# Decoder layer on one core: VectorE's share of the exponentials goes from 15 to 19 units a phase, by a quintic with a product made on GpSimd

## The chip, the cores and the metric

The kernel runs on one core of a Trainium2 chip. The metric is the device time of one execution in microseconds (us), as the median of several runs; lower is better.

## The reference

One decoder layer on `x` (1024 rows of 128) with a context `ctx` of 6404 rows of 128. Nearly all the time goes into the cross attention: 16 heads of depth 8, 1024 queries, 6404 keys.

```python
x = layernorm(x + attn(x, U))          # softmax(-|y_i - y_j|^2) @ x, y = x U
qh, kh, vh = heads(x @ Wq + bq), heads(ctx @ Wk + bk), heads(ctx @ Wv + bv)
attn = softmax(qh @ kh^T / sqrt(8))    # 16 x 1024 x 6404 exponentials
x = layernorm(x + (attn @ vh) @ Wo + bo)
x = layernorm(x + ffn_quantised(x))
```

## The kernel before

After a preparation (about 100 us: projections, keys split in three bf16 parts and written to DRAM), the attention runs in 8 **phases**: 4 groups of 4 heads times 2 halves of 512 queries. A phase walks over 17 **chunks** of 3 key tiles (`c` in 0 to 16). A chunk has 12 **units** of 128 keys x 512 queries, taken three at a time as 4 **blocks** (`t` or `s` in 0 to 3); the last chunk has 3 blocks, so a phase has 67. In this document "block 10" is the tenth after the phase's block 0, that is `c * 4 + t`.

For each block TensorE writes 3 units of scores into three of six PSUM banks (two sets, used in turn; `scores`, L1284), and ScalarE takes the exponential of the whole set in one instruction (`exponentials`, L710) into `probs`, a ring of 8 blocks in SBUF. TensorE later multiplies them with V, tile by tile (`values`, L1314). TensorE may start the scores of block b only when ScalarE has done block b-2, since both use the same banks (the wait on `probs_ready`).

One unit in some blocks isn't left to ScalarE: its instruction then covers 1024 columns and not 1536, and **VectorE** makes the third unit's exponentials by a polynomial. In the kernel before this is the third block (`E_BLOCK` is 2) of chunks 0 and 2 to 15: 15 units a phase. `take` rounds the scores (L960) and takes the fractional part (L966), both from PSUM; from then on the bank is free. `power` runs four steps of a polynomial (L979), then multiplies with a power of two and writes `probs` (L986). Every instruction covers 256 of the unit's 512 columns, so a unit is 14 instructions. **GpSimd** makes the power of two out of the rounded scores in one instruction (`powers`, L588), and copies V for each chunk into `v_op` (`stage`, L581), once TensorE has finished with the slot. VectorE waits at the end of a phase for the last values, adds and turns the accumulators (`add_acc`, `turn_acc`) and goes on. Each engine runs its own list in order; semaphores join them. SP's queue loads the keys for each chunk and the queries of each phase.

Of the kernel before, what the change touches and what calls it, by code (L numbers as in the profile page):

```python
# [22 lines left out]
F32 = mybir.dt.float32  # L23
# [6 lines left out]
P = 128  # L30
# [58 lines left out]

def decoder_layer(nc, x, ctx_in, U, Wq, bq, Wk, bk, Wv, bv, Wo, bo, clip_x, clip_down,  # L90
                  w_gate, w_up, w_down, out, score_limit=SCORE_LIMIT):
    stack = ExitStack()
    with stack:
# [64 lines left out]
        qf = sb("qf", [P, 2, HQ])  # L158
        qr = sb("qr", [P, 2, HQ])
# [41 lines left out]
        xq_t = sb("xq_t", [P, T], BF16)  # L201

# [34 lines left out]
        e_pow_ready = sem("e_pow_ready")  # L237
# [277 lines left out]
        def _(pool):  # L515
# [69 lines left out]
            def powers(ph, c):  # L585

                pool.wait_ge(e_step, E_STEPS * (e_count(ph, c) - 1) + 2)
                pool.tensor_scalar(e_pow[:], e_low(e_t[:]), float(2 ** 23), float(EXP2_LEAD),  # L588
                                   ALU.mult, ALU.add).then_inc(e_pow_ready, 1)

            for ph in range(PHASES):
                for c in range(NC):
                    m = ph * NC + c
                    stage(m % 2, m, c * CT, ph % NG * G)
                    if c != 1 and c < NC - 1:
                        powers(ph, c)
# [3 lines left out]
        def _(act):  # L600
# [113 lines left out]
            def shared(s):  # L714
                return BU * 512 - EW if s == E_BLOCK else BU * 512

            for ph in range(PHASES):
                f = ph * BPP
                for s in range(BPC):
                    exponentials(f + s, f + (s + 1 + AHEAD), shared(s))  # L720
                for s in range(BPC, 2 * BPC):
                    exponentials(f + s, f + (s + 1 + AHEAD))
                with act.Fori(0, E_UNITS // 2) as r:  # L723
                    for s in range(2 * BPC, 4 * BPC):
                        exponentials(f + s, r * (2 * BPC) + (f + s + 1 + AHEAD), shared(s % BPC))
# [788 lines left out]
```

## Time and profile before

| | |
|---|---|
| median of 3 runs | 834.43 us (834.39 to 834.64) |
| the profiled execution's own time | 833.03 us |
| its span (first to last instruction) | 831.3 us |
| busy in the span | TensorE 707.7, VectorE 689.5, ScalarE 736.0, GpSimd 174.9 us |
| one phase, start to start | 84.0 us |

The profiled execution is 1.4 us under the median of the runs; 1.7 us of it lie outside its span. Times in the views are from the span's start. A row that ends in "x6" in a timeline is six instructions merged, with the time from the first's start to the last's end.

### The profile page before, as it was taken

The numbers are of one execution on the slowest core, as the hardware profiler recorded it, in microseconds if no ns is written. First come the engines' busy times: TensorE is split into PE (matmuls) and PEld (weight loads), VectorE is DVE, ScalarE is ACT, GpSimd is POOL, SyncE is SP. The second block draws the span as 40 slices with busy tenths as digits, with TensorE's granted clock in tenths as the row PEclk, the third lists the DMA queues.
The fourth block names the chain that finished last, engine by engine and source line by source line (L and its number), as shares of the span: only waits on it lengthen the run. The fifth ranks groups of instructions, "written<-read, shape, count | busy, mean of one in ns | idle before, by whom it ended". The sixth has DMA issues, their size and how long they took to land.

```text
span 831.3 us, 38425 instructions
## 1 busy us (share of the span) xinstructions
PE 707.7 (85%) x15210; PEld 319.9 (38%) x15212; DVE 689.5 (83%) x1952; ACT 736.0 (89%) x650; POOL 174.9 (21%) x304
## 2 busy tenths in 40 slices
PE   6996679899899998899998999888899998899841
PEld 3445434443444344334443444344433443344321
DVE  3518767996999699969996999699978997899766
ACT  2436879999999999999999999999999999999741
POOL 2501511221222122212221222122212221222100
PEclk9998989999999999999999999999999999999965
DMA  3303521111111111111111111111111111111000
GB/s 105 83 25 107 170 86 37 37 43 44 38 36 45 42 37 38 43 43 38 36 44 43 36 37 40 44 38 35 40 48 35 37 37 49 37 36 38 14 1 26
DMA packets 36611, 38.41 MB, mean 46 GB/s; under 512 B 8430, under 2 KB 35088, under 8 KB 36512
## 3 DMA queue, kind: packets, MB, share of 16 engines
q1 hardware_dynamic: 35644, 36.59, 14.8%
q8 instruction: 65, 1.06, 0.5%
q10 hardware_dynamic: 868, 0.48, 0.2%
q14 instruction: 34, 0.28, 0.1%
HBM read 30.15 MB, written 6.42 MB: 44 GB/s over the span
## 4 chain that ended last, share of the span: by engine, by line
ACT 40%; issue 24%; PE 16%; SPq 10%; DVE 5%; DMA 3%; POOL 1%; ACTq 1%; POOLq 0%; DVEq 0%
ACT probs L710 39%; SPq L291 8%; PE ps L1314 6%; PE ps L1284 3%; PE ps L1213 2%; PE ps L1199 2%; DMA k_op<-k_parts_dram 2%; SPq L505 1%; DMA k_parts_dram<-k_parts 1%; PE ps L1162 1%; DVE stats L776 1%; PE ps L1449 1%; ACTq L723 1%; POOL k_parts L541 0%; DMA q_parts_dram<-q_parts 0%
## 5 line engine op out<-in xcount | busy, mean ns | idle before, releaser
L710 ACT ACTIVATE probs<-ps 128x1536 f32<-128x1536 f32 (+1 forms) x536 | 671.7, 1379 | 11.9 <-PE ps L1284 11.4
L1314 PE MATMUL ps<-probs,v_op 64*9 64x512 f32 (+1 forms) x8384 | 523.5, 494 | 13.8 <-DMA k_op<-k_parts_dram 9.1
L1284 PE MATMUL ps<-q_op,k_op 59*32 59x512 bf16 x6432 | 337.4, 382 | 60.7 <-ACT probs L710 56.4
L979 DVE SCALAR_TENSOR_TENSOR e_u<-e_u,e_f 128x256 f32<-128x256 f32 x720 | 259.2, 425 | 0.0
L1284 PEld LDWEIGHTS ps<-q_op,k_op 59*32 59x32 bf16 x6432 | 107.9, 90 | 331.5 <-issue 245.7
L1314 PEld LDWEIGHTS ps<-probs,v_op 64*9 64x9 f32 x8384 | 169.3, 86 | 90.2 <-issue 27.7
L588 POOL TENSOR_SCALAR e_pow<-e_t 128x512 int32<-128x512 int16 x120 | 74.4, 620 | 353.9 <-DVE e_t L960 353.9
L960 DVE TENSOR_SCALAR e_t<-ps 128x256 f32<-128x256 f32 x240 | 90.5, 418 | 60.5 <-PE ps L1284 51.3
L581 POOL COPY v_op<-v_all 128x108 f32<-128x108 f32 x136 | 68.3, 502 | 181.3 <-PE ps L1314 180.6
L979 DVE SCALAR_TENSOR_TENSOR e_u<-e_f 128x256 f32<-128x256 f32 x240 | 90.1, 416 | 0.2
L986 DVE SCALAR_TENSOR_TENSOR probs<-e_u,e_pow 128x256 f32<-128x256 f32 x240 | 89.6, 411 | 0.0
L966 DVE SCALAR_TENSOR_TENSOR e_f<-ps,e_t 128x256 f32<-128x256 f32 x240 | 89.2, 413 | 0.0
L541 POOL TENSOR_TENSOR k_parts<-probs,k_parts 128x384 bf16<-128x384 f32 x17 | 17.6, 1038 | 66.2 <-ACT k_parts L640 66.2
L667 ACT ACTIVATE probs<-ps,neg_n 128x1024 f32<-128x1024 f32 x8 | 8.9, 1113 | 16.8 <-PE ps L1213 16.8
L1162 PE MATMUL ps<-ctx_t,wk_turned 128*128 128x384 f32 x34 | 16.6, 571 | 6.3 <-ACT ctx_t L619 3.3
L1009 DVE STREAM_TRANSPOSE att_rows<-acc_t 128x512 f32<-128x512 f32 x7 | 5.0, 711 | 15.6 <-DMA o_t<-att_rows 15.6
L627 ACT ACTIVATE kf<-ps,bias_cols 128x384 f32<-128x384 f32 x17 | 9.8, 578 | 8.9 <-PE ps L1162 8.9
L1165 PEld LDWEIGHTS ps<-wv_sb,ctx_t 128*128 128x128 f32 x102 | 15.5, 208 | 5.2 <-issue 1.2
L1213 PE MATMUL ps<-y_rhs,y_lhs 64*128 64x512 f32 x32 | 15.6, 611 | 0.7 <-DVE v_all L811 0.7
L811 DVE TENSOR_TENSOR v_all<-ps,bv_bc 128x384 f32<-128x384 f32 (+1 forms) x17 | 9.4, 555 | 7.8 <-PE ps L1165 7.8
L640 ACT ACTIVATE k_parts<-probs 128x384 bf16<-128x384 f32 x17 | 8.8, 519 | 8.0 <-DVE probs L826 8.0
L1199 PE MATMUL ps<-probs,x_nat 128*128 128x512 f32 x32 | 15.6, 615 | 0.0
(177 smaller groups left out, 257.7 us busy)
## 6 DMA issues: line engine op xcount, KB each, us to landing
k_op<-k_parts_dram SPq DMA_DIRECT2D x544, 36.0 KB
k_parts_dram<-k_parts SPq DMA_DIRECT2D x17, 288.0 KB, 2.5
k_op<-k_parts_dram SPq DMA_DIRECT2D x272, 12.0 KB
ctx_nat<-in_ctx_dram SPq DMA_DIRECT2D x16, 192.0 KB, 2.6
q_op<-q_parts_dram SPq DMA_DIRECT2D x32, 48.0 KB
q_parts_dram<-q_parts SPq DMA_DIRECT2D x2, 384.0 KB, 3.4
x_nat<-in_x_dram SPq DMA_DIRECT2D x1, 512.0 KB, 3.9
o_t<-att_rows SPq DMA_DIRECT2D x28, 16.0 KB
```

Source lines behind the costliest of these rows:

```text
L291: sp.dma_start(k_op[W2 * r + a:W2 * r + a + DH * copies, slot, :, :].rearrange("p i t -> p (i t)"), bass.AP(src.tensor, starts[part][r], [ ...
L581: pool.tensor_copy(v_op[:, slot].rearrange("p j (h d) -> p j h d", h=G), v_all[:, bass.ds(tile, CT), head:head + G, :]).then_inc(v_staged, 1)
L588: pool.tensor_scalar(e_pow[:], e_low(e_t[:]), float(2 ** 23), float(EXP2_LEAD), ALU.mult, ALU.add).then_inc(e_pow_ready, 1)
L710: act.activation(probs[:, b % NP].rearrange("p u t -> p (u t)")[:, 0:columns], ps[:, bank:bank + BU, :].rearrange("p u t -> p (u t)")[:, 0 ...
L960: dve.tensor_scalar(e_t[:, cols], score, E_MIN, ROUND, ALU.max, ALU.add).then_inc(e_step, 1)
L966: dve.scalar_tensor_tensor(out=e_f[:, cols], in0=score, scalar=E_MIN, in1=e_low(e_t[:, cols]), op0=ALU.max, op1=ALU.subtract).then_inc(e_s ...
L979: dve.scalar_tensor_tensor(out=e_u[:, cols], in0=u[:, cols], scalar=a, in1=e_f[:, cols], op0=ALU.add, op1=ALU.mult).then_inc(e_step, 1)
L986: dve.scalar_tensor_tensor(out=probs[:, block % NP, BU - 1, 512 - EW + cols.start:512 - EW + cols.stop], in0=e_u[:, cols], scalar=EXP2[0], ...
L1199: last = pe.matmul(ps[:, 4 + b, :], x_nat[:, j, :], attn_e[:, j, HQ * b:HQ * b + HQ], start=(j == 0), stop=(j == TQ - 1), skip_group_check ...
L1213: last = pe.matmul(ps[:, 2 * (j % 2) + b, :], y_lhs[:, P * j:P * j + P], y_rhs[:, HQ * b:HQ * b + HQ], start=True, stop=True)
L1284: return pe.matmul(ps[a:a + P // G, bank, :], k_op[W2 * r:W2 * r + KR, kslot, i, P * j + a:P * j + a + P // G], q_op[W2 * r:W2 * r + KR, q ...
L1314: last = pe.matmul(ps[32 * k:32 * k + DH + 1, ACC[h], a:b], v_op[W2 * h:W2 * h + W2, slot, j, (DH + 1) * k:(DH + 1) * (k + 1)], probs[W2 * ...
```

## The change

The polynomial is another one, and its work is divided anew. With f the fraction and u0 = f + EXP2[0], GpSimd makes u = u0 * f, a quadratic; VectorE makes f' = (u + EXP2[2]) * f (`cube`), then f'' = (f' + EXP2[3]) * 2^n and (u + EXP2[1]) * f'' (`power`, now two steps). A unit is 10 VectorE instructions of 256 columns (was 14) and 3 GpSimd instructions of 512 (was 1): the power of two, `u0`, and the product, which reads two tiles. `e_f`, `e_u` and `e_pow` are doubled (the second set lies in `q_work`), `e_t` isn't.

A phase has 19 units, at the blocks listed by `E_AT`: block 0; then in each turn of 4 chunks, from chunk 2, blocks 2, 5, 8, 11 and 14 of the turn's 16; and blocks 58, 61 and 64. VectorE runs `take` of unit n, `power` of unit n-1, `cube` of unit n, and so on. TensorE reads values two chunks back for tile 2 and half of tile 1, one chunk back for the rest, and waits for the unit's semaphore `e_probs` where it reads it; before the scores of block b it waits for `e_taken` of a unit in block b-2.

```diff
+E_TURN = ((0, 2), (1, 1), (2, 0), (2, 3), (3, 2))
+E_AT = ([(0, 0)] + [(c + k, t) for c in range(E_FIRST, NC - 3, E_LOOP) for k, t in E_TURN] +
+        [(NC - 3, 2), (NC - 2, 1), (NC - 1, 0)])
...
-            def powers(ph, c):
-
-                pool.wait_ge(e_step, E_STEPS * (e_count(ph, c) - 1) + 2)
-                pool.tensor_scalar(e_pow[:], e_low(e_t[:]), float(2 ** 23), float(EXP2_LEAD),
+            def powers(ph, c, t):
+
+                n = e_count(ph, c, t)
+                f, u, pow2 = e_f[n % 2], e_u[n % 2], e_pow[n % 2]
+                if n > 2:
+
+                    pool.wait_ge(e_probs, E_AHEAD + 2 * (n - 2))
+                pool.wait_ge(e_rounded, 2 * n)
+                pool.tensor_scalar(pow2, e_low(e_t[:]), float(2 ** 23), float(EXP2_LEAD),
                                    ALU.mult, ALU.add).then_inc(e_pow_ready, 1)
+                pool.wait_ge(e_taken, 2 * n)
+                pool.tensor_scalar(u, f, EXP2[0], None, ALU.add).then_inc(e_square_ready, 1)
+                pool.wait_ge(e_square_ready, 2 * n - 1)
+                pool.tensor_tensor(u, u, f, ALU.mult).then_inc(e_square_ready, 1)
...
+            def cube(ph, c, t):
+
+                n = e_count(ph, c, t)
+                f, u = e_f[n % 2], e_u[n % 2]
+                dve.wait_ge(e_square_ready, 2 * n)
+                for cols in halves:
+                    dve.scalar_tensor_tensor(out=f[:, cols], in0=u[:, cols], scalar=EXP2[2],
+                                             in1=f[:, cols], op0=ALU.add, op1=ALU.mult
                                              ).then_inc(e_step, 1)
...
-                for i, a in enumerate(reversed(EXP2[1:])):
-                    u = e_f if i == 0 else e_u
-                    for n, cols in enumerate(halves):
...
+                for i, cols in enumerate(halves):
+                    dve.wait_ge(e_step, done + i + 1)
+                    dve.scalar_tensor_tensor(out=f[:, cols], in0=f[:, cols], scalar=EXP2[3],
+                                             in1=pow2[:, cols].bitcast(F32), op0=ALU.add, op1=ALU.mult
+                                             ).then_inc(e_step, 1)
+                for i, cols in enumerate(halves):
+                    dve.wait_ge(e_step, done + 2 + i + 1)
+                    dve.scalar_tensor_tensor(out=probs[:, block % NP, BU - 1, cols], in0=u[:, cols],
+                                             scalar=EXP2[1], in1=f[:, cols], op0=ALU.add, op1=ALU.mult
+                                             ).then_inc(e_probs, 1)
...
+                for n, at in enumerate(E_AT):
+                    take(ph, *at)
+                    if n > 1:
+                        power(ph, *E_AT[n - 1])
+                    elif n == 0 and ph:
+                        power(ph - 1, *E_AT[-1])
+                    cube(ph, *at)
...
+                    if c or s >= 2:
+                        wait_unit(e_taken, 0, ph, *((c, s - 2) if s >= 2 else (c - 1, s + 2)))
...
+                    elif s == 0:
+                        made(2, 1, a=HQ // 2)
+                    elif s == 1:
+                        made(2, 2)
+                    elif s == 2:
...
+                        made(1, 0, first=c == 1)
                     else:
-                        values(slot, f - BPC, 1, False, a=(s - 1) * (HQ // 2), b=s * (HQ // 2))
+                        made(1, 1, b=HQ // 2)
```

VectorE's list, one unit in the middle of a phase, before:

```order
L960 TENSOR_SCALAR e_t<-ps 128x256 [waits scores_done]
L960 TENSOR_SCALAR e_t<-ps 128x256
L966 SCALAR_TENSOR_TENSOR e_f<-ps,e_t 128x256 [waits e_step] x2
L979 SCALAR_TENSOR_TENSOR e_u<-e_f 128x256 [waits e_step] x2
L979 SCALAR_TENSOR_TENSOR e_u<-e_u,e_f 128x256 [waits e_step] x6
L986 SCALAR_TENSOR_TENSOR probs<-e_u,e_pow 128x256 [waits e_pow_ready,e_step] x2
```

The same place now, from one `take` to the next (`q_work` is the second set of the work tiles):

```order
L987 TENSOR_SCALAR e_t<-ps 128x256 [waits scores_done,e_pow_ready]
L987 TENSOR_SCALAR e_t<-ps 128x256
L991 SCALAR_TENSOR_TENSOR e_f<-ps,e_t 128x256 [waits e_rounded] x2
L1013 SCALAR_TENSOR_TENSOR q_work<-q_work 128x256 [waits e_step] x2
L1018 SCALAR_TENSOR_TENSOR probs<-q_work 128x256 [waits e_step] x2
L1001 SCALAR_TENSOR_TENSOR e_f<-e_u,e_f 128x256 [waits e_square_ready]
L1001 SCALAR_TENSOR_TENSOR e_f<-e_u,e_f 128x256
L987 TENSOR_SCALAR e_t<-ps 128x256 [waits scores_done,e_pow_ready]
```

The next `take` stands behind the `cube`, whose first instruction waits for GpSimd's product (`e_square_ready`); before, nothing between two takes waited for more than the power of two.

GpSimd's list in the middle of a phase, two chunks before:

```order
L581 COPY v_op<-v_all 128x108 [waits values_done,v_ready]
L588 TENSOR_SCALAR e_pow<-e_t 128x512 [waits e_step]
L581 COPY v_op<-v_all 128x108 [waits values_done,v_ready]
L588 TENSOR_SCALAR e_pow<-e_t 128x512 [waits e_step]
```

And now, two units:

```order
L591 COPY v_op<-v_all 128x108 [waits values_done,v_ready]
L603 TENSOR_SCALAR e_pow<-e_t 128x512 [waits e_rounded,e_probs]
L606 TENSOR_SCALAR e_u<-e_f 128x512 [waits e_taken]
L608 TENSOR_TENSOR e_u<-e_u,e_f 128x512 [waits e_square_ready]
L591 COPY v_op<-v_all 128x108 [waits values_done,v_ready]
L603 TENSOR_SCALAR q_work<-e_t 128x512 [waits e_rounded,e_probs]
L606 TENSOR_SCALAR q_work<-q_work 128x512 [waits e_taken]
L608 TENSOR_TENSOR q_work<-q_work 128x512 [waits e_square_ready]
```

Two instructions of 512 columns have come into each unit, and the second waits for the first's semaphore.

TensorE's list now, around the last block of one turn of four chunks and the first of the next (L1320 are scores, L1350 values; the registers' instructions carry the waits):

```order
L1363 REGISTER_ALU [waits e_taken,consts_ready]
L1320 MATMUL ps<-q_op,k_op 32x512 [waits probs_ready,consts_ready]
L1320 MATMUL ps<-q_op,k_op 32x512 x11
L1350 MATMUL ps<-probs,v_op 9x256 x8
L1363 REGISTER_ALU
L1320 MATMUL ps<-q_op,k_op 32x512 [waits probs_ready,consts_ready]
L1320 MATMUL ps<-q_op,k_op 32x512 x11
L1350 MATMUL ps<-probs,v_op 9x512 [waits e_probs,consts_ready]
L1350 MATMUL ps<-probs,v_op 9x512 x7
```

The same place before, where a chunk's last block ends with tile 2 of the chunk before:

```order
L1284 MATMUL ps<-q_op,k_op 32x512 [waits probs_ready,consts_ready]
L1284 MATMUL ps<-q_op,k_op 32x512 x11
L1327 REGISTER_ALU
L1314 MATMUL ps<-probs,v_op 9x512 [waits e_probs,consts_ready]
L1314 MATMUL ps<-probs,v_op 9x512 x7
L1327 REGISTER_ALU
L1327 REGISTER_ALU [waits e_step,consts_ready]
L1284 MATMUL ps<-q_op,k_op 32x512 [waits probs_ready,consts_ready]
```

The wait for a unit's values (`e_probs`) has moved from the chunk's fourth block to the second block of the chunk after, and stands between the scores of blocks 1 and 2.

## Rows read from the trace of the kernel before

**Rows 1.** The page's first part: busy time of each engine over the span.
```profile
PE 707.7 (85%) x15210; PEld 319.9 (38%) x15212; DVE 689.5 (83%) x1952; ACT 736.0 (89%) x650; POOL 174.9 (21%) x304
```

**Rows 2.** Windows: one stretch of 67 us inside the second phase.
```profile
core 0: us, PE busy (x) PEld busy (x) DVE busy (x) ACT busy (x) POOL busy (x), PEclk, DMA share, GB/s
198.00:265.00 67.00, 60.28 (x1524) 27.23 (x1512) 63.22 (x183) 66.94 (x54) 14.46 (x26) 1.00 0.13 38
```

**Rows 3.** Waits over the whole span: engine line, releaser: us in total, times, longest.
```profile
PE ps L1284 <- ACT probs L710: 56.4, 214, 1.4
DVE e_t L960 <- PE ps L1284: 51.3, 19, 6.1
```

**Rows 4.** Timeline of ScalarE: start, length, then the instruction; four in a row.
```profile
216.93 1.45 ACT L710 ACTIVATE probs<-ps 128x1536 f32<-128x1536 f32 x1
218.26 1.47 ACT L710 ACTIVATE probs<-ps 128x1536 f32<-128x1536 f32 x1
219.59 1.05 ACT L710 ACTIVATE probs<-ps 128x1024 f32<-128x1024 f32 x1
220.53 1.45 ACT L710 ACTIVATE probs<-ps 128x1536 f32<-128x1536 f32 x1
```

**Rows 5.** Timeline of VectorE: one unit and the start of the next.
```profile
219.19 0.76 DVE L960 TENSOR_SCALAR e_t<-ps 128x256 f32<-128x256 f32 x2
219.86 0.74 DVE L966 SCALAR_TENSOR_TENSOR e_f<-ps,e_t 128x256 f32<-128x256 f32 x2
...
221.19 2.17 DVE L979 SCALAR_TENSOR_TENSOR e_u<-e_u,e_f 128x256 f32<-128x256 f32 x6
223.28 0.75 DVE L986 SCALAR_TENSOR_TENSOR probs<-e_u,e_pow 128x256 f32<-128x256 f32 x2
224.13 0.76 DVE L960 TENSOR_SCALAR e_t<-ps 128x256 f32<-128x256 f32 x2
```

**Rows 6.** Timeline of GpSimd beside that unit.
```profile
220.03 0.62 POOL L588 TENSOR_SCALAR e_pow<-e_t 128x512 int32<-128x512 int16 x1 [2.90 <-DVE e_t L960]
221.56 0.51 POOL L581 COPY v_op<-v_all 128x108 f32<-128x108 f32 x1 [0.92 <-PE ps L1314]
```

**Rows 7.** Single lines: durations in ns as min/median/max, first and last start.
```profile
L581 POOL COPY v_op<-v_all x136: 272/517/2602, 102.7 to 779.9; 128x108 f32<-128x108 f32 x136
L541 POOL TENSOR_TENSOR k_parts<-probs,k_parts x17: 906/919/1296, 21.1 to 99.3; 128x384 bf16<-128x384 f32 x17
L826 DVE TENSOR_TENSOR probs<-kf,k_parts x17: 542/548/1124, 17.2 to 98.1; 128x384 f32<-128x384 f32 x17
```

**Rows 8.** Timeline of the preparation: a GpSimd and a VectorE instruction that overlap.
```profile
68.13 0.91 POOL L541 TENSOR_TENSOR k_parts<-probs,k_parts 128x384 bf16<-128x384 f32 x1 [31.93 <-ACT k_parts L640]
68.33 1.12 DVE L826 TENSOR_TENSOR probs<-kf,k_parts 128x384 f32<-128x384 f32 x1
```

**Rows 9.** Timeline of both engines in the seventh phase: the longest copy.
```profile
634.09 2.60 POOL L581 COPY v_op<-v_all 128x108 f32<-128x108 f32 x1 [0.84 <-PE ps L1314]
633.80 2.09 DVE L979 SCALAR_TENSOR_TENSOR e_u<-e_u,e_f 128x256 f32<-128x256 f32 x6
635.81 0.74 DVE L986 SCALAR_TENSOR_TENSOR probs<-e_u,e_pow 128x256 f32<-128x256 f32 x2
```

**Rows 10.** Groups of GpSimd: busy us, mean ns, idle before.
```profile
L588 POOL TENSOR_SCALAR e_pow<-e_t 128x512 int32<-128x512 int16 x120 | 74.4, 620 | 353.9 <-DVE e_t L960 353.9
L554 POOL MEMSET k_op<- 128x3072 bf16 x1 | 2.7, 2727 | 0.0
L571 POOL TENSOR_TENSOR x_bo<-x,bo_bc 128x1024 f32<-128x1024 f32 x1 | 2.4, 2357 | 0.0
```

**Rows 11.** Timeline of VectorE: the first unit of the third and of the fourth phase, and the second unit of the third.
```profile
277.54 0.76 DVE L960 TENSOR_SCALAR e_t<-ps 128x256 f32<-128x256 f32 x2 [4.13 <-PE ps L1284]
...
288.25 0.75 DVE L960 TENSOR_SCALAR e_t<-ps 128x256 f32<-128x256 f32 x2 [1.73 <-PE ps L1284]
...
361.55 0.76 DVE L960 TENSOR_SCALAR e_t<-ps 128x256 f32<-128x256 f32 x2 [4.14 <-PE ps L1284]
```

**Rows 12.** Timeline of TensorE: scores, a full tile of values, the next scores.
```profile
219.87 0.61 PE L1284 MATMUL ps<-q_op,k_op 59*32 59x512 bf16 x12 [0.30 <-ACT probs L710]
220.14 1.21 PE L1314 MATMUL ps<-probs,v_op 64*9 64x512 f32 x16
221.05 0.61 PE L1284 MATMUL ps<-q_op,k_op 59*32 59x512 bf16 x12
```

More of the change, by code:

```diff
@@ L593, in _ @@
                     m = ph * NC + c
-                    stage(m % 2, m, c * CT, ph % NG * G)
-                    if c != 1 and c < NC - 1:
-                        powers(ph, c)
+                    for t in range(BPC):
+                        if t == 2:
+                            stage(m % 2, m, c * CT, ph % NG * G)
+                        if (c, t) in E_AT:
+                            powers(ph, c, t)
         @block.scalar
@@ L712, in exponentials, with chunk @@
                                ACT.Exp, scale=1.0 / LOG2E).then_inc(probs_ready, 1)
-            def shared(s):
-                return BU * 512 - EW if s == E_BLOCK else BU * 512
-            for ph in range(PHASES):
[L718 to L725, printed above, removed]
-                for s in range((NC - 1) * BPC, BPP):
-                    exponentials(f + s, f + (s + 1 + AHEAD))
+            def chunk(ph, c, i=None):
+                f = ph * BPP + c * BPC
+                for t in range(LAST_BPC if c == NC - 1 else BPC):
+                    count = f + t + 1 + AHEAD
+                    exponentials(f + t, count if i is None else i * (E_LOOP * BPC) + count,
+                                 BU * 512 - EW if (c, t) in E_AT else BU * 512)
+            for ph in range(PHASES):
+                for c in range(E_FIRST):
+                    chunk(ph, c)
+                with act.Fori(0, (NC - 3 - E_FIRST) // E_LOOP) as i:
+                    for c in range(E_FIRST, E_FIRST + E_LOOP):
+                        chunk(ph, c, i)
+                for c in range(NC - 3, NC):
+                    chunk(ph, c)
             act.wait_ge(pe_tail, TAIL_ATT_T)
@@ L1326, in at @@
                 def at(count, step):
-                    return count if i is None else pe.to_reg(i * (reach * step) + count)
+                    return count if i is None else pe.to_reg(i * step + count)
                 def wait(signal, count):
@@ new lines, in made @@
+                def made(back, j, a=0, b=HQ, count=1, first=False):
+                    ph_v, c_v = (ph, c - back) if c >= back else (ph - 1, c - back + NC)
+                    if ph_v < 0:
+                        return
+                    if j == 0:
+                        wait(v_staged, at(m - back + 1, KS))
+                    if a == 0:
+                        for t in range(BPC):
+                            if (t * BU + BU - 1) // G == j:
+                                wait_unit(e_probs, E_AHEAD, ph_v, c_v, t)
+                    values((m - back) % 2, ph_v * BPP + c_v * BPC, j, c_v == NC - 1, count, first, a, b)
@@ L1358, in chunk @@
+                    if c == 0:
+                        if s < 2:
+                            made(2, s + 1, count=2 - s)
+                        else:
+                            made(1, s - 2, count=s - 1)
+                    elif c == 1 and s < 2:
+                        if s == 0:
+                            made(2, 2)
                     elif s == 0:
+                        made(2, 1, a=HQ // 2)
+                    elif s == 1:
+                        made(2, 2)
+                    elif s == 2:
@@ L1387, in project_out @@
                 last.then_inc(pe_tail, 1)
+            last_m = PHASES * NC - 1
+            pe.wait_ge(e_probs, E_AHEAD + 2 * (E_UNITS * PHASES - 1))
+            for j in range(1, CT):
+                values((last_m - 1) % 2, BLOCKS - LAST_BPC - BPC, j, False, count=3 - j)
             pe.wait_ge(o_written, 16 * G * NG)
```

136 lines of the change are left out of this document (62 added, 74 removed).

## The prediction

> **What bounds the kernel now.** I read the page's busy times first [rows 1]: ScalarE, TensorE and VectorE lie close together, so a share of the span decides nothing. The windows show the inside of a phase [rows 2]: ScalarE is busy for 66.94 of 67.00 us, VectorE 63.22, TensorE 60.28, GpSimd 14.46, TensorE's granted clock 1.00, the upper of its levels, 2.4 GHz. The waits say the same from the other side [rows 3]: TensorE's scores wait for ScalarE 214 times, VectorE waits for scores 19 times, mostly at a phase's start. So ScalarE bounds every phase. Its pace is in the timeline [rows 4]: starts 1.33 us apart behind an instruction of 1536 columns, 0.94 behind one of 1024. A unit taken from it saves 0.39 us. VectorE is just behind: a unit of 14 instructions every 4.94 us, 0.335 us each [rows 5]. GpSimd's two instructions in that time cost nothing [rows 6].
>
> **What the change removes.** Four more units a phase leave ScalarE: 4 x 0.39 = 1.56 us a phase, 12.5 us over 8 phases, if ScalarE stays the bound. VectorE goes from 15 x 14 = 210 to 19 x 10 = 190 instructions a phase, so by count it has room too.
>
> **What it adds: a chain through GpSimd.** Between two takes VectorE must now pass the cube, which waits for a GpSimd product made from this unit's fraction. The time from take to take can't be less than this chain. With ScalarE as the bound there are, over three blocks with one shortened, 2 x 1.33 + 0.94 = 3.6 us for it, and from block 14 to 18 4.94 us.
>
> The two new GpSimd instructions have no row of their own. The product: two-input instructions took 2.36 us for 1024 columns and 0.91 (the undisturbed ones) for 384, 2.27 ns a column, so 512 take 0.91 + 0.29 = 1.20 us [rows 7, 10]. The addition of a constant: nearest is the power of two, 0.62 us for the same 512 columns [rows 10]. Bounds: a memset's rate, 2.73 us for 3072 columns, gives 0.45 below; the two-input price 1.20 above. I take 0.62.
>
> The GPSIMD Engine Reference of the Trainium skill (section 3.1) gives one-input bodies 1.03 cycles an element, about 0.44 us for 512 at its 1.2 GHz, as an estimate; the trace's 0.62 for such an instruction is longer. By the page's figure the sum below would be 26 us less.
>
> **What the two engines do to each other.** VectorE's instruction with two SBUF inputs took 0.55 us alone and 1.12 when a GpSimd instruction had started 0.2 us before it: that ended at 69.04, VectorE's at 69.45, as if it had begun when GpSimd ended, 0.41 us for 384 columns, so 0.27 for 256 [rows 7, 8]. The other way round, the copy takes 0.27 alone and 0.52 beside the polynomial's steps, and the six steps around it take 2.17 instead of 2.09 [rows 5, 6, 7, 9]. So a VectorE instruction that reads two SBUF tiles and a GpSimd instruction that reads SBUF exclude each other for nearly their whole length. In before this cost 0.08 us a chunk. After, cube and power (six instructions a unit) read two SBUF tiles, and so they exclude GpSimd's 0.62 and 1.20. Only take, which reads PSUM, runs beside GpSimd, and GpSimd's addition can't start until take is done.
>
> The copy's 0.27 kept VectorE out for some 0.15 (0.08 lost, and the gap of 0.335 - 0.27 used), so I count 0.12 us less than a GpSimd instruction's length as exclusion. The cycle, in order: take 4 x 0.335 = 1.34; power's first 0.33, in which GpSimd's addition becomes ready (fraction seen at 1.42, start 0.08 later as behind the rounding [rows 5, 6]) and waits; addition 0.50; power's second 0.27; product 1.08; power's last two and cube's two, 4 x 0.335 = 1.34. That is 4.86. The copy of V, now in four of five units, becomes ready while GpSimd is in the product and then takes its turn among these: 0.8 x 0.08 = 0.06. **4.9 us a unit.** That is above the 3.6 us, and above the 4.94 us only where four blocks lie between. So VectorE with GpSimd sets the pace, ScalarE waits.
>
> Two more waits follow. (1) power of unit n ends 4.2 us after take of n+1. TensorE reads unit 11 of a turn in block 17, before the scores of block 18. Its scores of block 16 follow take of block 14 (1.42 + 0.1 + 0.6 = 2.1), those of 17 at 3.0, then it waits to 4.2, values 0.6, scores 0.6 [rows 12]: take of block 18 at 5.5 and not 4.9. 0.6 us, three times a phase. (2) At a phase's start block 64's values are read after the scores of block 2, so again at 4.2 behind take of block 0; values 0.6, scores 0.6: 5.4; ScalarE runs six blocks to 5.4 + 6 x 1.34 = 13.4, scores 0.6: the second unit (block 10) is taken 14.0 us after the first. VectorE's work on the accumulators, some 4 us, lies inside.
>
> **Sum.** From block 10 to the next phase's block 0 there are 18 intervals of 4.9 = 88.2, plus 3 x 0.6 = 1.8, plus 14.0: 104.0 us. Before: 84.0 [rows 11]. +20.0 a phase, 160 over 8. At the end the last unit's power and two tiles of values come behind ScalarE's end: +3. Against the profiled execution's 833.0: 996; the median was 1.4 above it: **998 us**. The 12.5 us of ScalarE are in this sum as nothing: it is idle for about a fifth of the phase.
>
> **Bounds.** Addition at 0.45, copy free, neither of the two extra waits: 18 x 4.67 + 12.1 = 96.2, gives 934. Addition at 1.20 gives 1082.
>
> **Rivals.** (a) *GpSimd starved.* One copy took 2.60 us: it waited until eight back-to-back steps had ended [rows 7, 9]. If GpSimd's addition isn't let in between power's four instructions, the cycle is 1.34 + 1.34 + 0.50 + 0.2 + 1.08 + 0.1 + 0.67 = 5.23, a phase 110, the time 1047. Against it: the median copy, 0.52, got in after one step. The SBUF — State Buffer page of the Trainium skill (section "SBUF: two separate sides") says that whichever starts first holds the shared pair for its whole instruction and the other blocks; by that a waiting GpSimd instruction goes next. The 2.60 us copy doesn't agree, the median does. 0.12.
>
> (b) *No exclusion for these shapes.* Then 1.42 + 0.08 + 0.62 + 0.09 + 1.20 + 0.09 + 0.67 = 4.17 us; 18 x 4.17 + 12.1 = 87.2, +3.2 a phase: 861. It still loses since 4.17 is over ScalarE's average, (84.0 - 13.0) / 18 = 3.94 at break-even. Against it stands [rows 8]. 0.08.
>
> (c) *Faster.* GpSimd's two instructions take together less than 3.94 - 2.35 = 1.59 us, undisturbed (mine are 1.82), so ScalarE stays the bound and the 12.5 us come: 822. Needs both (b) and faster instructions than any row. 0.04. That the product saves VectorE nothing at all, no change: 0.01.
>
> (d) *More than I counted*: the addition at its upper price, or TensorE at 1.2 GHz for stretches, since it would be busy 60.3 x 84 / 104, some 73% of a window where it now has 90% at clock 1.00 [rows 2]. Values and scores would then lengthen both extra waits. 0.08, 1065 and up.
>
> **Chances.** The ledger with GpSimd let in between (934 to 1035): 0.67; (a) 0.12; (d) 0.08; (b) 0.08; (c) 0.04; no change 0.01. The range 920 to 1065 holds the first two and a little of (d). This kernel's runs differ by 0.03%, so 0.2% is what can be told from no change. Faster 0.04, same 0.01, slower 0.95.
>
> **What would show it.** VectorE's takes 4.9 us apart inside a phase; idle time of ScalarE behind TensorE's scores of some 20 us a phase, and those waiting for VectorE's fraction; VectorE's step behind the product of 1.2 us or more instead of 0.42; GpSimd's addition near 0.75 with its wait, its product near 1.2; GpSimd about 2.5 us busy a unit. The forecast is wrong if VectorE's steps keep 0.42 us beside GpSimd's product, if the product takes under 1 us, or if takes follow each other in 3.6 us.

## The result, and the profile after

| | before | after |
|---|---|---|
| median | 834.53 us (834.39 to 834.76, 4 runs) | 1025.91 us (1023.92 to 1028.12, 4 runs) |
| profiled execution, its span | 833.03, 831.3 us | 1023.92, 1022.2 us |
| first takes of phases, apart | 90.0, then 83.9 to 85.6 us | 108.4 to 109.0 us |

The ratio is 1.229, with an interval of 1.2266 to 1.2313. Slower was forecast, with 998 us in 920 to 1065; the time lies 28 us above the forecast.

The page's first part, the answer to [rows 1], and its fourth, the shares of the chain that ended last:

```profile
PE 749.9 (73%) x15212; PEld 314.0 (31%) x15212; DVE 704.5 (69%) x1792; ACT 742.8 (73%) x650; POOL 591.9 (58%) x640
...
POOL 38%; DVE 27%; PE 19%; issue 9%; ACT 6%; POOLq 0%; DVEq 0%; ACTq 0%
```

No engine is above 73% now, and yet GpSimd, the least busy of the four, holds the most of the chain. That is how a round trip between two engines looks on a page: neither is full, since each stands while the other works. The windows say it of 60 us inside one phase (columns as in [rows 2], where ScalarE was busy all the time):

```profile
340.00:400.00 60.00, 44.91 (x1036) 18.67 (x1036) 44.70 (x114) 45.59 (x37) 42.37 (x44) 0.94 0.09 27
```

The waits, answering to [rows 3] (us in total, times, longest), name the round trip and its followers:

```profile
ACT probs L731 <- PE ps L1320: 189.0, 167, 2.2
DVE q_work L1001 <- POOL q_work L608: 110.1, 76, 3.1
DVE e_f L1001 <- POOL e_u L608: 108.4, 76, 3.1
PE ps L1320 <- DVE q_work L991: 87.4, 65, 2.2
PE ps L1320 <- DVE e_f L991: 83.0, 65, 2.0
PE ps L1350 <- DVE probs L1018: 21.2, 42, 1.3
```

VectorE's cube (L1001) waits 218.5 us for GpSimd's product, in all 152 units, 1.44 us each. TensorE's scores wait 170 us for the take that stands behind that cube, and ScalarE waits 189 us for the scores. It is one wait told three times. The two timelines show one unit whole, VectorE first:

```profile
401.41 0.74 DVE L987 TENSOR_SCALAR e_t<-ps 128x256 f32<-128x256 f32 x2
402.07 0.74 DVE L991 SCALAR_TENSOR_TENSOR q_work<-ps,e_t 128x256 f32<-128x256 f32 x2
402.74 1.21 DVE L1013 SCALAR_TENSOR_TENSOR e_f<-e_f,e_pow 128x256 f32<-128x256 f32 x2
403.87 0.75 DVE L1018 SCALAR_TENSOR_TENSOR probs<-e_u,e_f 128x256 f32<-128x256 f32 x2
405.95 0.80 DVE L1001 SCALAR_TENSOR_TENSOR q_work<-q_work 128x256 f32<-128x256 f32 x2 [1.33 <-POOL q_work L608]
```

and GpSimd beside it:

```profile
402.31 0.62 POOL L603 TENSOR_SCALAR q_work<-e_t 128x512 int32<-128x512 int16 x1 [1.44 <-DVE e_t L987]
403.01 1.55 POOL L606 TENSOR_SCALAR q_work<-q_work 128x512 f32<-128x512 f32 x1
404.64 1.28 POOL L608 TENSOR_TENSOR q_work<-q_work 128x512 f32<-128x512 f32 x1
```

The addition (L606) starts 1.60 us after the take, behind the power of two that is in GpSimd's way until then. It takes 1.55 us, not the 0.62 that I had counted. Then 0.08, the product 1.28, 0.03, and the cube's 0.72 up to the next take: 1.60 + 1.55 + 0.08 + 1.28 + 0.03 + 0.72 = **5.26 us**, the distance of takes inside a phase. The power's four instructions (L1013, L1018) end at 404.62, beside the addition, and VectorE stands idle while the product runs. Over the whole span the addition's mean is 1.54 us and the product's 1.28, 152 of each.

Takes in VectorE's timeline, answering to [rows 11]: the first unit of the first, the third, the fourth and the last phase, and the second unit of the third:

```profile
101.76 0.74 DVE L987 TENSOR_SCALAR e_t<-ps 128x256 f32<-128x256 f32 x2
...
319.10 0.74 DVE L987 TENSOR_SCALAR e_t<-ps 128x256 f32<-128x256 f32 x2
...
333.04 0.75 DVE L987 TENSOR_SCALAR e_t<-ps 128x256 f32<-128x256 f32 x2 [3.58 <-PE ps L1320]
...
427.75 0.74 DVE L987 TENSOR_SCALAR e_t<-ps 128x256 f32<-128x256 f32 x2
...
862.83 0.74 DVE L987 TENSOR_SCALAR e_t<-ps 128x256 f32<-128x256 f32 x2
```

The third phase is 108.65 us long: 13.94 to the second unit, then 18 intervals of 5.26 on average; the three over four blocks are 5.30 to 5.32. (In the last phase the second unit comes 15.4 us after the first, in the first 13.7.)

The first and the last phase of the kernel before began here:

```profile
103.65 0.76 DVE L960 TENSOR_SCALAR e_t<-ps 128x256 f32<-128x256 f32 x2 [0.98 <-PE ps L1284]
...
700.98 0.76 DVE L960 TENSOR_SCALAR e_t<-ps 128x256 f32<-128x256 f32 x2 [4.82 <-PE ps L1284]
```

So seven phases took 597.3 us before and 761.1 after, +163.7; the first take came 1.9 us earlier, and from the last phase's first take to the end it went from 130.3 to 159.4, +29.1. Together +190.9, all of the difference of the two profiled executions.

### The profile page after: what moved, and what is told of

The parts are those of the page before. It is cut to its first block, busy times and chain, and to the rows that moved or that the text cites. A ratio compares the mean times of both kernels' runs of the same rounds, so it can differ in the third digit from the quotient of the medians.

```text
span 1022.2 us, 38544 instructions
## 1 busy us (share of the span) xinstructions
PE 749.9 (73%) x15212; PEld 314.0 (31%) x15212; DVE 704.5 (69%) x1792; ACT 742.8 (73%) x650; POOL 591.9 (58%) x640
## 4 chain that ended last, share of the span: by engine, by line
POOL 38%; DVE 27%; PE 19%; issue 9%; ACT 6%; POOLq 0%; DVEq 0%; ACTq 0%
DVE e_t L987 10%; POOL q_work L606 9%; POOL e_u L606 8%; PE ps L1350 8%; POOL q_work L608 7%; POOL e_u L608 7%; ACT probs L731 5%; PE ps L1320 4%; POOL q_work L603 3%; DVE e_f L1001 3%; POOL e_pow L603 3%; DVE q_work L1001 3%; DVE probs L1018 2%; PE ps L1249 1%; PE ps L1235 1%
## 5 line engine op out<-in xcount | busy, mean ns | idle before, releaser
L1350 PE MATMUL ps<-probs,v_op 64*9 64x512 f32 (+1 forms) x8384 | 546.1, 516 | 23.0 <-DVE probs L1018 21.2
L1320 PE MATMUL ps<-q_op,k_op 59*32 59x512 bf16 x6432 | 352.5, 397 | 200.8 <-DVE q_work L991 87.4
L1320 PEld LDWEIGHTS ps<-q_op,k_op 59*32 59x32 bf16 x6432 | 117.0, 93 | 480.5 <-issue 355.1
L1350 PEld LDWEIGHTS ps<-probs,v_op 64*9 64x9 f32 x8384 | 166.8, 89 | 137.8 <-issue 73.1
L1001 DVE SCALAR_TENSOR_TENSOR q_work<-q_work 128x256 f32<-128x256 f32 x152 | 60.7, 438 | 110.1 <-POOL q_work L608 110.1
L1001 DVE SCALAR_TENSOR_TENSOR e_f<-e_u,e_f 128x256 f32<-128x256 f32 x152 | 60.7, 438 | 108.4 <-POOL e_u L608 108.4
L606 POOL TENSOR_SCALAR q_work<-q_work 128x512 f32<-128x512 f32 x76 | 117.3, 1544 | 6.0
L606 POOL TENSOR_SCALAR e_u<-e_f 128x512 f32<-128x512 f32 x76 | 117.3, 1543 | 6.0
L608 POOL TENSOR_TENSOR e_u<-e_u,e_f 128x512 f32<-128x512 f32 x76 | 97.1, 1278 | 6.3
L608 POOL TENSOR_TENSOR q_work<-q_work 128x512 f32<-128x512 f32 x76 | 97.0, 1277 | 6.3
L1013 DVE SCALAR_TENSOR_TENSOR q_work<-q_work 128x256 f32<-128x256 f32 x152 | 90.7, 635 | 0.0
L1013 DVE SCALAR_TENSOR_TENSOR e_f<-e_f,e_pow 128x256 f32<-128x256 f32 x152 | 90.2, 632 | 0.0
L1018 DVE SCALAR_TENSOR_TENSOR probs<-e_u,e_f 128x256 f32<-128x256 f32 x152 | 56.7, 411 | 0.0
L1018 DVE SCALAR_TENSOR_TENSOR probs<-q_work 128x256 f32<-128x256 f32 x152 | 56.7, 411 | 0.0
L991 DVE SCALAR_TENSOR_TENSOR q_work<-ps,e_t 128x256 f32<-128x256 f32 x152 | 56.2, 408 | 0.0
```

The costliest lines, as they stand in the source:

```text
L606: pool.tensor_scalar(u, f, EXP2[0], None, ALU.add).then_inc(e_square_ready, 1)
L608: pool.tensor_tensor(u, u, f, ALU.mult).then_inc(e_square_ready, 1)
L991: dve.scalar_tensor_tensor(out=f[:, cols], in0=ps[:, bank, cols], scalar=E_MIN, in1=e_low(e_t[:, cols]), op0=ALU.max, op1=ALU.subtract).th ...
L1001: dve.scalar_tensor_tensor(out=f[:, cols], in0=u[:, cols], scalar=EXP2[2], in1=f[:, cols], op0=ALU.add, op1=ALU.mult).then_inc(e_step, 1)
L1013: dve.scalar_tensor_tensor(out=f[:, cols], in0=f[:, cols], scalar=EXP2[3], in1=pow2[:, cols].bitcast(F32), op0=ALU.add, op1=ALU.mult).then ...
L1018: dve.scalar_tensor_tensor(out=probs[:, block % NP, BU - 1, cols], in0=u[:, cols], scalar=EXP2[1], in1=f[:, cols], op0=ALU.add, op1=ALU.mu ...
```

## Experiments

Two things were open: why the addition takes 1.55 us, and whether the two engines exclude each other at all, since the cycle of 5.26 adds up without it. On the addition: either it is the price of this form of instruction, or VectorE keeps it out. On the cycle: exclusion is real but hidden, because the power lies beside the slow addition; or there is none, and the chain's lengths are all; or VectorE's own work bounds it. Each experiment ran beside the kernel before on the same chip: 832.38 us (one run) for the first four, 834.96, 835.28 and 835.13 (medians of 14 to 17 runs) for the others. The first four and e10 have one run each; their differences are read inside the timelines. Where a run's text names one interval of takes, it is the usual one inside a phase.

**e1_prices**: the disputed prices by themselves. Behind the end of the kernel before, GpSimd runs a row of instructions of 512 columns, twice with VectorE idle, twice beside a stream of VectorE steps that read two SBUF tiles.

```diff
+                priced.step(pool.tensor_scalar(pb, pa, 28.2, None, ALU.add))
+                priced.step(pool.tensor_scalar(pb, pa, 28.2, 1.5, ALU.add, ALU.mult))
+                priced.step(pool.tensor_scalar(pb, pa, 28.2, 1.5, ALU.mult, ALU.add))
+                priced.step(pool.tensor_scalar(pb, pa, 28.2, None, ALU.mult))
+                priced.step(pool.tensor_tensor(pc, pb, pa, ALU.mult))
+                priced.step(pool.tensor_tensor(pc, pa, pa, ALU.mult))
...
```

> The kernel before, with a price list behind its end: when all its work is done, GpSimd runs eleven instructions of 512 columns on spare tiles, each waiting for the one before, twice with VectorE idle and twice beside 60 VectorE instructions of 256 columns that read two SBUF tiles. Its time means nothing. Theory S (the new addition is slow by itself): the addition of a constant to 512 f32 columns takes about 1.5 us with VectorE idle, the product about 1.27. Theory X (the prediction's: the addition is as short as the power of two, and is kept waiting by VectorE): the addition takes about 0.6 us alone and 1.5 only beside VectorE's stream. Both: the int16 to int32 form takes 0.62.

Its time, 891.41 us, says nothing, as the work is added. The timeline of GpSimd, VectorE idle, in the order of the diff (L608 to L613; the third, 0.62 us too, is left out):

```profile
827.82 1.50 POOL L608 TENSOR_SCALAR v_all<-v_all 128x512 f32<-128x512 f32 x1 [44.96 <-DVE res L816]
829.41 0.62 POOL L609 TENSOR_SCALAR v_all<-v_all 128x512 f32<-128x512 f32 x1
...
830.81 1.50 POOL L611 TENSOR_SCALAR v_all<-v_all 128x512 f32<-128x512 f32 x1
832.39 1.26 POOL L612 TENSOR_TENSOR v_all<-v_all 128x512 f32<-128x512 f32 x1
833.73 1.04 POOL L613 TENSOR_TENSOR v_all<-v_all 128x512 f32<-128x512 f32 x1
```

The first of them beside VectorE's stream, the stream's first 12 steps beside GpSimd, and its last 25, when GpSimd has ended:

```profile
851.97 1.66 POOL L608 TENSOR_SCALAR v_all<-v_all 128x512 f32<-128x512 f32 x1 [0.20 <-POOL v_all L618]
...
851.86 9.23 DVE L1160 SCALAR_TENSOR_TENSOR v_all<-v_all 128x256 f32<-128x256 f32 x12 [24.20 <-POOLq L623]
...
877.75 11.47 DVE L1160 SCALAR_TENSOR_TENSOR v_all<-v_all 128x256 f32<-128x256 f32 x25
```

A scalar instruction with one operation takes 1.50 us, with two operations 0.62, in either order. I had taken the price of the power of two, which has two. Beside VectorE's stream each of them is only 0.04 to 0.16 longer (the product 1.35): contention doesn't explain 1.55. The stream itself, in which each step waits for the one before, gets 12 steps in 9.23 us, 0.77 each; once GpSimd has ended they follow 0.46 apart. So the two engines do keep each other out, and it is VectorE that pays. Step by step: the one under way beside a scalar instruction takes 0.71 us and not 0.42, whether that instruction is the long or the short one, and the next two beside the long one take 0.42 again; beside a product of two tiles a step takes 1.37. The long scalar instruction keeps VectorE out no longer than the short one.

**e2_no_add**: GpSimd makes u = f * f; the addition of EXP2[0] is left out of the computation.

```diff
-                pool.tensor_scalar(u, f, EXP2[0], None, ALU.add).then_inc(e_square_ready, 1)
-                pool.wait_ge(e_square_ready, 2 * n - 1)
-                pool.tensor_tensor(u, u, f, ALU.mult).then_inc(e_square_ready, 1)
+                pool.tensor_tensor(u, f, f, ALU.mult).then_inc(e_square_ready, 2)
```

> The changed kernel without GpSimd's addition: the product is f * f, so the polynomial lacks one coefficient. Takes now 5.26 us apart. If a serial chain alone set the pace (fraction, addition, product, cube) it would be 5.26 - 1.63 = 3.63 us, ScalarE would be the bound again and the time 820 to 830. If exclusion counts as well: the product can't run beside power's last three instructions, so 1.34 + 0.39 + 1.15 + 5 x 0.335 = 4.55 us a unit, a phase 95.8, the time about 928. Theory X with an addition of 0.6 us and 0.9 us of waiting: about 4.6, the same 930.

913.45 us. VectorE, then GpSimd, in one unit:

```profile
407.87 0.76 DVE L985 TENSOR_SCALAR e_t<-ps 128x256 f32<-128x256 f32 x2 [0.15 <-PE ps L1318]
...
409.20 1.65 DVE L1011 SCALAR_TENSOR_TENSOR q_work<-q_work 128x256 f32<-128x256 f32 x2
...
412.19 0.74 DVE L985 TENSOR_SCALAR e_t<-ps 128x256 f32<-128x256 f32 x2
...
409.48 1.09 POOL L606 TENSOR_TENSOR e_u<-e_f 128x512 f32<-128x512 f32 x1
```

The square again starts 1.61 us after the take. By the chain alone the next take could follow at 1.61 + 1.09 + 0.03 + 0.72 = 3.45, under ScalarE's three blocks; it follows at 4.32. The power's first two instructions take 1.65 us instead of 0.74: the second waits until the square ends. So with the addition gone the exclusion shows. 110 us of the profiled 1023.92 come back, near what was expected with exclusion (928 us in all, 4.55 a unit) and far from the 820 to 830 of the chain alone.

**e3_one_step**: the power's first step is left out (the factor 2^n with it); two VectorE instructions a unit less.

```diff
-E_STEPS = 4
+E_STEPS = 2
...
-                    dve.scalar_tensor_tensor(out=f[:, cols], in0=f[:, cols], scalar=EXP2[3],
-                                             in1=pow2[:, cols].bitcast(F32), op0=ALU.add, op1=ALU.mult
-                                             ).then_inc(e_step, 1)
```

> The changed kernel with power's first step (the multiplication with the power of two) left out, so VectorE has 8 instructions a unit and two fewer that exclude GpSimd; the output lacks that factor. Theory S: VectorE's steps lie beside the slow addition, the cycle stays at 5.2 and the time at 1015 to 1026. Theory X: GpSimd's addition and product get in earlier, 5.26 - 0.67 = 4.6 us, the time about 930.

1025.73 us, nothing gained, and takes still 5.27 apart:

```profile
403.07 0.74 DVE L987 TENSOR_SCALAR e_t<-ps 128x256 f32<-128x256 f32 x2
...
407.62 0.80 DVE L1001 SCALAR_TENSOR_TENSOR q_work<-q_work 128x256 f32<-128x256 f32 x2 [2.01 <-POOL q_work L608]
408.34 0.74 DVE L987 TENSOR_SCALAR e_t<-ps 128x256 f32<-128x256 f32 x2
```

The cube's wait grew from 1.33 to 2.01 us, by the 0.67 that was cut. VectorE's own work is not the bound.

**e4_late_cube**: the cube of unit n stands behind the take of unit n+1, so that the chain no longer lies between two takes.

```diff
+                        cube(ph, *E_AT[n - 1])
...
-                    cube(ph, *at)
```

> The changed kernel with the cube of unit n moved behind the take of unit n+1, in front of its power: all work stays, only the serial chain from take to take is cut. Without exclusion GpSimd's own work would be the bound, 0.62 + 1.55 + 1.28 + 0.22 + waits 0.3 = 4.0 us a unit, the time about 845. With exclusion of the parts in which GpSimd reads (0.5 + 0.66 + 1.15 + 0.12) and VectorE's six two-input instructions (2.0) it is 4.4 to 4.6 us, the time about 925. If the addition excludes VectorE for its whole length, 5.3 us or more, the time about 1030. Theory X expects about 4.6.

1024.29 us, where a large gain was expected: a miss. Over three blocks the cycle does fall, to 4.88, but not over four:

```profile
399.62 0.74 DVE L987 TENSOR_SCALAR e_t<-ps 128x256 f32<-128x256 f32 x2
...
404.50 0.74 DVE L987 TENSOR_SCALAR e_t<-ps 128x256 f32<-128x256 f32 x2
...
407.63 1.82 DVE L1018 SCALAR_TENSOR_TENSOR probs<-q_work 128x256 f32<-128x256 f32 x2
411.12 0.76 DVE L987 TENSOR_SCALAR e_t<-ps 128x256 f32<-128x256 f32 x2 [1.67 <-PE ps L1323]
```

A unit's values are now ready later, 4.95 us after the next take, and TensorE waits for them before it writes the next scores: 6.62 us here, and 15.7 at the phase's start. These are the two extra waits of the prediction; the first had been small in the kernel after (5.3 over four blocks), the second is longer than its 13.94. They take back the 0.38 that each shorter interval gives: phases are 108.6 to 109.6 us long (the first 106.3), against 108.4 to 109.0. Taking the chain off one path put its length on another.

**e5_two_op**: the addition gets a second operation that does nothing, a multiplication by 1.

```diff
-                pool.tensor_scalar(u, f, EXP2[0], None, ALU.add).then_inc(e_square_ready, 1)
+                pool.tensor_scalar(u, f, EXP2[0], 1.0, ALU.add, ALU.mult).then_inc(e_square_ready, 1)
```

> The changed kernel with one edit: GpSimd's addition gets a second operation, a multiplication by 1.0, since in the price list that form took 0.62 us and the form with one operation 1.49. All values stay the same. If only the serial chain counts: 5.26 - 0.93 = 4.33 us a unit and about 915 us. If exclusion counts as in the prediction's ledger (power's second instruction waits for the addition, its last two and the cube for the product): 4.75 to 4.9 us a unit, about 990 us.

1016.39 us (1012.49 to 1022.93, 4 runs), 1.2163 times the kernel before (1.2084 to 1.2243). GpSimd and VectorE in one unit:

```profile
407.08 0.67 POOL L606 TENSOR_SCALAR e_u<-e_f 128x512 f32<-128x512 f32 x1
407.83 1.32 POOL L608 TENSOR_TENSOR e_u<-e_u,e_f 128x512 f32<-128x512 f32 x1
...
400.50 0.74 DVE L987 TENSOR_SCALAR e_t<-ps 128x256 f32<-128x256 f32 x2
...
405.48 0.74 DVE L987 TENSOR_SCALAR e_t<-ps 128x256 f32<-128x256 f32 x2
...
407.94 1.83 DVE L1018 SCALAR_TENSOR_TENSOR probs<-q_work 128x256 f32<-128x256 f32 x2
...
411.43 0.76 DVE L987 TENSOR_SCALAR e_t<-ps 128x256 f32<-128x256 f32 x2 [0.99 <-PE ps L1320]
```

The addition lost 0.88 us, the cycle only 0.29 (4.98 from 400.50 to 405.48). The product now falls on the power's last two instructions, which take 1.83 us and not 0.75, and the cube no longer waits at all. This is the unit as the prediction drew it, and its 4.9 us is 0.08 short of it. The time was still missed: with exclusion about 990 us had been expected. As the power ends later, TensorE's wait for values has grown from 21.2 us in 42 waits to this:

```profile
PE ps L1350 <- DVE probs L1018: 128.7, 112, 2.4
```

Over four blocks the interval is 5.95 to 6.06 (5.3 in after), the second unit mostly comes 16.5 us after the first (13.94), and a phase is 107 to 108.5 us. So the shorter cycle is mostly lost again outside it.

**e10_two_op_one_step** puts e3's cut on top of e5, to separate exclusion from chain (again without the factor 2^n).

> e5 (the addition with two operations) with power's first step left out, the same cut that changed nothing in e3 (the output lacks the power of two). If exclusion between power and the product sets e5's 4.97 us, the cut takes two VectorE instructions of 0.335 us off the path: 4.3 us a unit inside a turn and about 930 us. If only the serial chain counted, the cut would change nothing again: 4.97 us and about 1010 us.

904.18 us; takes 4.44 apart:

```profile
402.97 0.74 DVE L987 TENSOR_SCALAR e_t<-ps 128x256 f32<-128x256 f32 x2
...
406.69 0.80 DVE L1001 SCALAR_TENSOR_TENSOR e_f<-e_u,e_f 128x256 f32<-128x256 f32 x2 [1.17 <-POOL e_u L608]
407.41 0.74 DVE L987 TENSOR_SCALAR e_t<-ps 128x256 f32<-128x256 f32 x2
```

The same two instructions were worth nothing in e3 and 0.54 us a unit here, and 112 us in all with the shorter waits for values. A chain by itself can't do that: in e5 the power stood in the product's way, in e3 it had a gap. Hidden exclusion is what both runs fit; 4.44 is also what the chain alone adds up to here (1.61 + 0.67 + 0.08 + 1.33 + 0.03 + 0.72).

**e6_vector_product**: VectorE makes (f + EXP2[0]) * f itself, in one instruction per half; GpSimd keeps only the power of two. Still 19 units; 12 instructions a unit.

```diff
-                pool.tensor_scalar(u, f, EXP2[0], None, ALU.add).then_inc(e_square_ready, 1)
-                pool.wait_ge(e_square_ready, 2 * n - 1)
-                pool.tensor_tensor(u, u, f, ALU.mult).then_inc(e_square_ready, 1)
...
+                    dve.scalar_tensor_tensor(out=u[:, cols], in0=f[:, cols], scalar=EXP2[0],
+                                             in1=f[:, cols], op0=ALU.add, op1=ALU.mult
+                                             ).then_inc(e_square_ready, 1)
```

> The changed kernel with the same polynomial, but VectorE makes the product itself, in two instructions (f + a) * f; GpSimd is left with the power of two. 12 VectorE instructions a unit, 19 units. Both theories: no wait for GpSimd is left, 12 x 0.335 = 4.02 to 4.1 us a unit, over ScalarE's 3.9 on average, so some 855 us (848 to 865): two VectorE instructions cost less than the wait for GpSimd, but 19 units are still too many.

866.79 us (865.71 to 867.28, 4 runs), 2 us over the range expected; ratio 1.0359 (1.0303 to 1.0415). Two takes:

```profile
406.61 0.76 DVE L983 TENSOR_SCALAR e_t<-ps 128x256 f32<-128x256 f32 x2 [0.86 <-PE ps L1322]
...
410.68 0.74 DVE L983 TENSOR_SCALAR e_t<-ps 128x256 f32<-128x256 f32 x2
```

Two VectorE instructions, 0.67 us, do what cost 1.1 us of blocked VectorE or 1.4 us of waiting. So 159 of the 191 us lie in GpSimd's having the addition and the product. What is left is VectorE's own pace, 4.07 to 4.13 us for three blocks in which ScalarE needs 3.6.

**e7 to e11** look for a version that gains. All have 16 units a phase, mostly four blocks apart, where ScalarE gives VectorE 4.94 us (at block 2 of chunks 0 and 2 to 15 and block 1 of chunk 16). TensorE also gets one more wait, behind chunk 1, for the values of the phase's first unit.

```diff
-E_TURN = ((0, 2), (1, 1), (2, 0), (2, 3), (3, 2))
+E_TURN = ((0, 2), (1, 2), (2, 2), (3, 2))
...
-         [(NC - 3, 2), (NC - 2, 1), (NC - 1, 0)])
+         [(NC - 3, 2), (NC - 2, 2), (NC - 1, 1)])
```

e7_vector_product_16 is e6 with these units:

> As e6, with 16 units a phase, four blocks apart (blocks 2, 10, 14 and so on to 62, and 65), so that 4.0 to 4.1 us of VectorE lie under ScalarE's 4.94. ScalarE should be the bound everywhere and lose one unit of 0.39 us a phase against the kernel before: 834.5 - 3.1 = 831.4 us. If a wait appears at the phase's start it is 832 to 835.

840.81 us (12 runs), ratio 1.0079 (1.0046 to 1.0113): missed. Intervals inside are 4.95, as before, but the second unit comes 12.13 us after the first, before it was 10.71. At that place TensorE waits 1.77 us for the last unit's exponentials, and ScalarE for the scores:

```profile
367.32 15.40 ACT L727 ACTIVATE probs<-ps 128x1536 f32<-128x1536 f32 x12 [1.72 <-PE ps L1322]
```

e8_two_op_16 is e5 with them, GpSimd making the product:

> As e5 (product on GpSimd, addition with two operations), with the 16 units of e7. The chain's 4.3 us or the ledger's 4.75 to 4.9 both lie under ScalarE's 4.94 a unit: 831 to 835 us by both; above 840 would mean that the cycle is longer than either says.

988.93 us (6 runs), ratio 1.1821 (1.1756 to 1.1887): missed by far. The cycle of e5, 4.98, nearly fits 4.94, but nearly every interval is 6.05 to 6.07:

```profile
445.81 1.07 PE L1350 MATMUL ps<-probs,v_op 64*9 64x512 f32 x16 [1.21 <-DVE probs L1018]
...
441.35 0.76 DVE L987 TENSOR_SCALAR e_t<-ps 128x256 f32<-128x256 f32 x2 [1.09 <-PE ps L1320]
...
447.42 0.76 DVE L987 TENSOR_SCALAR e_t<-ps 128x256 f32<-128x256 f32 x2 [1.09 <-PE ps L1320]
```

The power of unit n-1 ends 4.3 us after take n, TensorE reads it at 4.46, and only then writes the scores of unit n+1: 4.46 + 1.6 = 6.06. In e5 the same wait came three times a phase. The chain is closed a second time, over the values.

e9_power_at_once is e7 with the last unit's power made before the next phase begins:

> As e7 (product on VectorE, 16 units), but the phase's last unit gets its power at once and not behind the next phase's first take. In e7 TensorE waited 1.77 us for it in the fourth block of each phase and ScalarE then stood still for 1.72 us. With the wait gone a phase should be 84.0 - 0.4 = 83.6 to 83.9 us and the time 831 to 834, against 839 to 841 of e7 and 834.4 of the kernel before. If the stall has another cause the time stays at 840.

839.48 us (9 runs), ratio 1.0058 (1.0036 to 1.008), missed: in the fourth phase ScalarE still stands 1.31 us, only 7.6 us behind the phase's first take and not 4.4 as in e7. It stands behind TensorE's values of that place, which have an idle 1.40 us ahead of them whose end the trace doesn't name; the accumulators were the suspect, and e11 moves them.

e11_in_order makes each unit's power right behind its cube, and adds the accumulators before the phase's first power:

> As e9 (product on VectorE, 16 units), but every unit gets its power right behind its cube, before the next take, and the accumulators are added before the first unit's power. In e9 TensorE still waited 1.40 us a phase for the addition of the accumulators and the phase's first take came 0.3 to 0.5 us late. If these are all that is left, a phase is 83.6 to 83.8 us and the time 2 to 3 us under the kernel before on the same chip (ratio 0.996 to 0.998); if the 16th unit can't be hidden at the phase's end, the ratio stays at 1.00 or above.

836.08 us (12 runs), ratio 1.0009 (0.9975 to 1.0043): level with the kernel before. ScalarE runs over the fourth phase's start at 359.47 without a gap (the row merges instructions of both lengths):

```profile
354.73 30.52 ACT L727 ACTIVATE probs<-ps 128x1024 f32<-128x1024 f32 x24
```

What the 16th unit should have given, 0.39 x 8 = 3.1 us, isn't seen in the medians, whose runs spread from 832.15 to 842.74. The traced executions show a part of it: the seven phases took 595.5 us against 597.3 before, but from the last phase's first take to the end it was 131.8 against 130.3, and ScalarE's waits for scores were 13.5 against 11.4. One execution of each can't say more. No version here beat the kernel before. That the quintic saves instructions is true, but fewer instructions on an engine that didn't bound give nothing, and the units that could have used them come three blocks apart, where even 12 instructions don't fit.

## Why the prediction was right, and where it was off

- **The mechanism**, right: the product's round trip lies between two takes and is longer than ScalarE's three blocks. VectorE with GpSimd sets the pace, ScalarE waits (189 us; I said some 20 a phase, it was 24). The bound is another one than the ledger's, though. The ledger adds up work and exclusion on a VectorE that never stands inside a unit; the trace shows a serial chain over both engines, and VectorE standing for 1.33 us of it.
- **Addition 0.62**: wrong, and it is the step that failed. It measured 1.55 us (1.50 undisturbed, e1), outside even my bounds of 0.45 to 1.20. I took the nearest row by columns and type, but that instruction had two operations and this one has one. The GPSIMD Engine Reference of the Trainium skill (section 3.1) gives one price (1.03 cycles an element) for k ≤ 2, so for one and for two operations as I read it, about 0.44 us as an estimate; the rows differ from it by 0.2 and 1.1 us.
- **Product 1.20**: right, 1.28 in place and 1.26 alone (e1).
- **The exclusion**: real (e1, e2, e5, e10), and for a scalar addition of 0.62 the cycle of the ledger would have held: 4.9 against the 4.98 of e5. In the kernel as it is, it costs almost nothing. The power's second instruction was held up for 0.4 us (0.82 long) and the rest ran beside the slow addition, ending 0.06 us after it. The ledger would have put the addition's whole length on VectorE. The SBUF — State Buffer page of the Trainium skill (section "SBUF: two separate sides") says that the first holds the other off for its whole length: the product does so (e5), the addition of 1.55 us doesn't.
- **The signs named**: the takes, ScalarE's idle time and the product came near enough. VectorE's step of 1.2 us or more behind the product didn't, since VectorE stands while the product runs; it is there in e5 (1.49). GpSimd's addition was to show near 0.75 with its wait and took 1.55, and GpSimd is busy for 3.45 us a unit without the copy, not 2.5.
- **Cycle 4.9**: 5.26. The addition was 0.93 too short, the exclusion of some 0.6 was counted and not paid. Two errors against each other left 0.36. The right answer on a cycle was partly luck, and e5, which removes one of them, shows it.
- **Extra wait (1), 0.6 three times a phase**: 0.06. The power ends 3.2 us after the next take and not 4.2, since nothing holds it up beside the addition; values and scores then lie inside the cycle. In e5 (5.95 to 6.06, a cycle of 4.98) the wait is there, and longer than drawn: 1.0 to 1.1 us and not 0.6.
- **Extra wait (2), second unit at 14.0**: 13.94, right in sum and by luck in its parts. In the third phase TensorE reads the values at 3.35 behind the take and not at 4.2; ScalarE goes on 1.55 later and not 1.2; from there to the last scores it is 8.31 and not 8.0, and to the take 0.73 and not 0.6.
- **Phase 104.0**: 108.65, from 18 x 0.36 = 6.5 more (the remains of extra wait (1) in it), 1.8 less.
- **+20.0 a phase on 84.0**: the base was too short. Phases before were 90.0, 83.9, 84.0, 83.9, 84.7, 85.6 and 85.2 us; I had read two. The mean of 85.3 makes the increase 9 us smaller over seven phases, which hid a part of the error. The 28 us in full: seven phases now take 33 more than 7 x 104.0, before they took 9 more than 7 x 84.0, the last phase to the end is 6 over the forecast's 20 + 3, the start 1.9 earlier: 33 - 9 + 6 - 1.9 = 28. (The forecast's own sum is 997.4 and not 998.)
- **Rival (a)**, GpSimd starved, 5.23 and 1047 (its phase of 110 gives 1045): close in number, wrong in cause. The addition starts 0.08 us behind the power of two, at once. **(b)**, no exclusion: e2 and e10 speak against it. **(c)** needed the pair under 1.59; it is 2.83. **(d)**: the addition went over its upper price, and yet the time stayed under 1065, as the exclusion had been charged too high. TensorE's granted clock fell: 0.94 in the window above against 1.00 (2.4 GHz throughout), 0.944 over the span against 0.967. From 344 to 358 us it was 0.88 and takes lie 5.26 and 5.27 apart, from 196 to 203 it was 1.00 and they lie 5.22 and 5.27 apart, so it cost nothing that shows.

## What to carry to other kernels

A step given to another engine is priced by its round trip between two steps that must follow each other, not by what the engines have free: draw the unit with both engines' lines, and close every loop in it, the one over later readers too (e4, e8). Price an instruction by a row of the same form, the number of its operations included, and put one in a kernel of its own before you trust the nearest row. Before giving a two-input product to GpSimd, count what VectorE loses while it runs: 1.1 us in e5, against 0.67 for making it itself. And take a phase's length over all phases before a difference is multiplied by their number.

## What the runs showed of the hardware

- GpSimd's scalar instruction on 512 columns of f32: 1.50 us with one operation, 0.62 with two (add and multiply in either order). A second operation that does nothing made it 0.88 us shorter in the kernel. Why isn't known.
- A product of one tile with itself takes 1.04 us, of two tiles 1.26.
- The one-operation instruction, though twice as long, kept VectorE out for only a part of its length, and no longer than the short form does (a step of 0.71 us beside either in e1): in the unit shown at the top three of the power's four instructions ended during its 1.55 us, and the fourth 0.06 us behind it. Beside e5's product (1.32 us, 407.83 to 409.15) only the one under way ended; the two of L1018 ended behind it (the first took 1.49 us).
- Against GpSimd the stream of VectorE's steps lost far more (e1: 0.46 to 0.77 us from step to step) than GpSimd's instructions (0.04 to 0.16 us each).
